# Rows of ones made pair by pair, batch 1 prepared from step 0 on, and the last experts' first weights loaded inside attention

## The reference

```
x = x + 0.5 * ffn(layernorm(x))     # first expert phase
x = x + attn(layernorm(x))
x = x + 0.5 * ffn(layernorm(x))     # second expert phase, same weights
```

## Time and profile before

| | us |
|---|---|
| median of 3 runs | 2451.97 |
| runs | 2429.93 to 2452.05 |
| profiled execution | 2452.92 |
| its span, first to last instruction | 2451.1 |
| TensorE busy | 2177.5 (89%) |
| VectorE, ScalarE, GpSimd busy | 1740.6, 1730.3, 976.2 |
| mean granted TensorE clock | 0.91 |

### The profile page before, as it was taken

One profiled execution on the slowest core, in us unless ns is written; L12 is line 12 of the kernel. 1 busy time (PEld: TensorE's weight loads), 2 busy tenths in 40 slices (PEclk: granted clock), 3 DMA queues, 4 the chain that ended last, 5 costly groups with the idle time before them and its releaser, 6 DMA issues.

```text
span 2451.1 us, 36414 instructions
## 1 busy us (share of the span) xinstructions
PE 2177.5 (89%) x12974; PEld 1153.8 (47%) x12974; DVE 1740.6 (71%) x2555; ACT 1730.3 (71%) x3390; POOL 976.2 (40%) x1157
## 2 busy tenths in 40 slices
PE   5749964579999999999999999999999999964997
PEld 5748853344344434434443443444444334224896
DVE  5636754368888888798888778878888988203774
ACT  5846654128888788788878878877887877634663
POOL 3754512271264256239227514832741111112442
PEclk8569986569999999999999999999999999666998
DMA  5725420514235334344333444432362340103431
GB/s 201 264 88 181 152 73 35 103 35 96 54 64 120 58 76 105 71 58 105 97 57 85 101 76 73 90 94 37 84 122 41 78 62 16 51 9 130 139 121 61
DMA packets 144901, 218.29 MB, mean 89 GB/s; under 512 B 32224, under 2 KB 100954, under 8 KB 144464
## 3 DMA queue, kind: packets, MB, share of 16 engines
q1 hardware_dynamic: 135504, 199.01, 34.6%
q0 software_dynamic: 9216, 16.95, 2.0%
HBM read 129.59 MB, written 84.80 MB: 87 GB/s over the span
## 4 chain that ended last, share of the span: by engine, by line
PE 73%; DVE 10%; POOL 5%; ACT 5%; issue 4%; DMA 2%; SPq 0%; POOLq 0%; DVEq 0%; ACTq 0%
PE PS L780 18%; PE PS L764 17%; PE PS L747 11%; PE PS L692 6%; DVE NMX L1302 5%; PE PS L568 4%; PE PS L724 3%; POOL buf L1425 2%; PE PS L661 2%; PE PS L662 2%; PE PS L663 2%; PE PS L645 2%; PE PS L647 2%; PE PS L600 2%; PE PS L646 2%
## 5 line engine op out<-in xcount | busy, mean ns | idle before, releaser
L1302 DVE TENSOR_REDUCE NMX<-PS 128x1 f32<-128x1024 f32 x1024 | 1224.5, 1219 | 300.7 <-PE PS L747 294.9
L998 ACT ACTIVATE PB<-PS 128x512 f32<-128x512 f32 x2048 | 1103.4, 605 | 250.9 <-PE PS L764 243.4
L764 PE MATMUL PS<-QF,KF 51*128 51x512 f32 x2048 | 814.6, 473 | 12.1 <-ACT PB L998 7.4
L747 PE MATMUL PS<-KF,QF 49*128 49x512 f32 x2048 | 725.1, 451 | 47.8 <-DVE NMX L1302 35.6
L764 PEld LDWEIGHTS PS<-QF,KF 51*128 51x128 f32 x2048 | 334.8, 189 | 573.6 <-ACT PB L998 292.8
L780 PE MATMUL PS<-PB,V 128*17 128x512 f32 x4096 | 559.4, 619 | 0.2
L747 PEld LDWEIGHTS PS<-KF,QF 49*128 49x128 f32 x2048 | 315.7, 190 | 181.9 <-DVE NMX L1302 116.1
L1406 POOL TENSOR_TENSOR RS<-VE,NEGH 128x8 f32<-128x8 f32 x24 | 40.2, 1676 | 404.8 <-DVE VE L1096 404.8
L1229 DVE TENSOR_TENSOR HLR<-HL,HHR 128x512 fp32r<-128x512 f32 x128 | 88.7, 693 | 91.8 <-ACT HHR L928 91.8
L661 PE MATMUL PS<-W2H,HLR 128*128 128x256 f32 x512 | 142.8, 279 | 0.0
L663 PE MATMUL PS<-W2H,HHR 128*128 128x256 f32 x512 | 141.5, 276 | 0.0
(11 more groups left out here) (171 smaller groups left out, 3303.5 us busy)
## 6 DMA issues: line engine op xcount, KB each, us to landing
W<-in_w SPq DMA_DIRECT2D x32, 1024.0 KB, 8.1
QF<-qs SPq DMA_DIRECT2D x192, 128.0 KB, 4.7
KF<-qs SPq DMA_DIRECT2D x192, 128.0 KB, 7.5
qs<-HI SPq DMA_DIRECT2D x64, 256.0 KB, 2.1
qs<-R1R SPq DMA_DIRECT2D x64, 256.0 KB, 2.4
buf<-ZT SPq DMA_DIRECT2D x16, 520.0 KB, 9.9
BUF<-buf SPq DMA_DIRECT2D x16, 520.0 KB, 8.4
PX<-x2d SPq DMA_DIRECT2D x8, 1024.0 KB, 5.5
```

Source lines behind the costliest of these rows:

```text
L747: m = e.matmul(PS[:, 2 * i + half, :], QF[k][at:at + ROWS_S, p * SEQ + ti * 128:p * SEQ + ti * 128 + 128], KF[k][at:at + ROWS_S, p * SEQ + ...
L764: e.matmul(PS[:, bank, :], KF[k][at:at + ROWS_ST, p * SEQ + sbk * 128:p * SEQ + sbk * 128 + 128], QF[k][at:at + ROWS_ST, p * SEQ + th * 51 ...
L998: e.activation(PB[j % 3][:, h * 512:(h + 1) * 512], PS[:, place["e", tile], :], ACT.Exp).then_inc(e_out, 1)
L1302: e.tensor_reduce(NMX[:, u % 2, at:at + 1], PS[:, 2 * i:2 * i + 2, :], AX.XY, ALU.max, negate=True).then_inc(s_max, 1)
```

## The change

1. Ones. The three pairs get their rows from a generator `ones()`: pair 0 at once, pairs 1 and 2 in step 60 of batch 0's preparation. `load_unit(u)` waits for the ones of its own pair instead of `load_unit(0)` for all. The memsets of V17 write the 17th column only.
2. Batch 1. All engines begin its preparation with base 0 instead of -12. Its `load_unit(4)` comes in step 53 instead of 52.
3. Weights. SP issues `load_w(8)` and `load_w(9)` in step 492, after waits for all users of the scratch under them. ScalarE and VectorE convert W1 and W2 of expert 8 in step 534 (ScalarE behind a wait for the last `weigh`) instead of after the loop and at the head of `experts(1)`.

The diff, cut to its core (the line for batch 1 stands the same way in TensorE's, ScalarE's, VectorE's and GpSimd's programs):

```diff
                 if u >= 3:
                     e.wait_ge(e_full, 64 * (u - 2))
+                else:
+                    e.wait_ge(set_act, 2 * u + 2)
...
                 if b:
-                    yield EARLY + 52
+                    yield EARLY + 52 if b > 1 else 53
                     load_unit(4 * b)
...
-            e.wait_ge(set_act, 6)
             load_unit(0)
             for n in range(NS + LAST + 1):
                 b, r = divmod(n, BATCH)
                 if n == 0:
-                    side.begin(-EARLY, before(1))
+                    side.begin(0, before(1))
...
                 side.run(n)
-
-            e.wait_ge(e_out, 64 * NU)
-            e.wait_ge(pv_full, 16 * NU)
-            e.wait_ge(rope_out, 8 * NB)
-            load_w(NE)
-            load_w(NE + 1)
+                if n == NS - 20:
+
+                    e.wait_ge(sq_sum, 8 * NB)
+                    e.wait_ge(rope_out, 8 * NB)
+                    e.wait_ge(sp_full, 8 * NB)
+                    for i in range(2):
+                        e.wait_ge(st_q[i], 128 * NB)
+                    load_w(NE)
+                    load_w(NE + 1)
             experts(1)
...
                 if n == 0:
-                    prepare(side, -EARLY, 1, pre_x, values, split)
+                    prepare(side, 0, 1, pre_x, values, split)
...
-                if ph:
-                    split_w2(NE)
                 gathered(NE * ph)
...
-            for k in range(3):
-                for t in (QF[k], KF[k]):
-                    e.copy(t[32:64, :], ONES[32:64, 0:1].to_broadcast([32, 2048]))
-                    e.copy(t[96:128, :], ONES[96:128, 0:1].to_broadcast([32, 2048])).then_inc(set_act, 1)
+            def ones():
+                for k in range(3):
+                    for t in (QF[k], KF[k]):
+                        e.copy(t[32:64, :], ONES[32:64, 0:1].to_broadcast([32, 2048]))
+                        e.copy(t[96:128, :], ONES[96:128, 0:1].to_broadcast([32, 2048])).then_inc(set_act, 1)
+                    yield VALUES_AT[3] + 1
+
+            side.begin(0, ones())
             prepare(side, 0, 0, pre_x, values, split)
...
                 side.run(n)
-
-            e.wait_ge(pv_full, 16 * NU)
-            split_w1(NE)
+                if n == NS + LAG + LATE:
+
+                    e.wait_ge(pv_full, 16 * NU)
+                    split_w1(NE)
+                    split_w2(NE)
+
...
-            own.out(e.memset(V17[0][:, :, :, :], 1.0))
-            own.out(e.memset(V17[1][:, :, :, :], 1.0))
+            own.out(e.memset(V17[0][:, :, :, 16:17], 1.0))
+            own.out(e.memset(V17[1][:, :, :, 16:17], 1.0))
...
-            split_w1(NE)
+                if n == NS + LAG + LATE:
+                    split_w1(NE)
+                    split_w2(NE)
+
```

More of the change, by code:

```diff
@@ L1347, in vector_program @@
                 if n == 0:
-                    prepare(side, -EARLY, 1, pre_x, split)
+                    prepare(side, 0, 1, pre_x, split)
                 if r == BATCH - EARLY and b + 2 < NB:
```

## The result

| | before | after |
|---|---|---|
| median of 20 runs, us | 2449.5 | 2423.1 |
| runs, us | 2429.9 to 2452.4 | 2404.9 to 2433.1 |
| ratio after / before, 95% interval | | 0.9887 (0.9865 to 0.9909) |
| profiled execution, us (span) | 2452.9 (2451.1) | 2421.0 (2419.2) |

The median falls by 26 us. The runs of a kernel fall into two groups some 20 us apart, and this must be seen first, since it is where about half of the gap comes from. Before: 19 runs at 2446.7 to 2452.4 (mean 2449.7) and one at 2429.9. After: 11 runs at 2421.0 to 2433.1 (mean 2428.0) and 9 at 2404.9 to 2409.7 (mean 2408.0). Upper against upper and lower against lower, the kernels differ by about 22 us.

The account below looks back on a forecast made before the run. TensorE was taken as 73% of the chain of waits, so gains come only where it stands still. Terms -11.3 - 22.0 + 10.3 + 9 + 2.5 - 3.0 - 1.3 + 1.0 = -14.8, from 2452.9 to 2438 us; range 2421 to 2449.

Parts of the forecast that it names:

- rival (a): Step 36: GpSimd finishes the split before SP needs it, so no new wait for MT; 2426.6 us, chance 0.12.
- the 1% that was called likeliest: Whole kernel: a change within about 1% (24.5 us, line at 2427.5) counts as the same; chance 0.73.
- Ones: Start of batch 0's preparation: eight of twelve copies leave ScalarE's queue head, which then waits for GpSimd; gain 11.3 us.
- Fill: Steps 0 to 19 of attention: 65.1 us instead of 87.05 with batch 1 prepared later, -22.0.
- the 20 x 2.53: Steps 0 to 19: twenty undisturbed steps of 2.53 us each, paced by two 1.2 us maxima on VectorE.
- Moved work, stop and clock: Behind the fill: six projections and two splits +10.3, SP's queue stopping TensorE in step 36 +9, low clock +2.5.
- (c): After the stop in step 36 the clock does not come back; slower, 2483 us, chance 0.05.
- Weights and passage: Passage into the second expert phase, weights loaded in step 492: scatter -3.0, BUF -1.3, reciprocal's store +1.0.
- Scatter: Passage: the last scatter, no longer beside the weight loads, lands in 2.8 us instead of 5.85; -3.0.
- BUF: Passage: the BUF load took 5.32 us; between 0 and half of it gained, taken as -1.3.
- RC's store: Step 534: conversion ahead of unit 31's reciprocal delays its store from 2180.84 to 2181.9; +1.0.
- If the changed kernel's median falls there: Rival: whole at another level, likeliest place the last 20 steps at low clock; 2416 us, chance 0.10.

Follow-up runs that it names:

- experiment 5: Ones alone, and batch 1's preparation from step 0 alone, each on the kernel before with idle score matmuls (chip B): 2436.7 and 2437.9 us.
- experiment 3: Changed kernel with one store of batch 1's preparation (split half 0, j = 1) due one step later, chip A: 2426.15 us.
- experiment 4: Changed kernel with idle matmuls, batch 1 at base 4: 2416.4 us (chip B); with batch 2's x2 load also three steps later, no stop: 2388.85 us (chip C).
- Experiment 1: Four idle matmuls per step, steps 513 to 531, added to before and changed kernels: 2427.5 and 2406.5 us (chip A), 2426.2 and 2406.9 (chip C).

## Why the prediction was right or wrong

The size was wrong: 14 us below the median of before were forecast, 26 measured. The median lies in the range, but by luck: the range reached down that far for rival (a), no wait for MT, and the wait came. The measured ratio of 0.9887 lies past the 1% that was called likeliest, though the interval (up to 0.9909) does not exclude it.

**Ones**, forecast -11.3: -11.0 (100.2 to 89.2). ScalarE waits for GpSimd as said, and the moved copies cost nothing (experiment 5: steps 0 to 63 unchanged).

**Fill**, forecast -22.0: -25.0. Mis-sized were the terms around the 20 x 2.53. The load and statistics lengthened steps 0 to 4 by 3.2 us, not 4.4. The transposes lengthened steps 9 to 12 by 1.9, not 4.35, because VectorE's maxima pace these steps and TensorE has room beside them: I charged TensorE's time in a stretch that I had myself called paced by VectorE. The projections took 6.5, not 5.7.

**Moved work, stop and clock**, forecast 10.3 + 9 + 2.5 = 21.8: steps 20 to 63 are 21.8 longer. The stop is 8.45, the low clock behind it 3.2 (steps 36 to 39, 14.6 against 11.4 in experiment 3), which leaves 10.1 for the moved work. The kernel of experiment 4 without a stop supports it: 12.0 for eight projections and two splits, where these terms give 11.2. The Trainium skill ("TensorE: Matmul & The Clock Gate", Terms) puts the penalty of a low clock at the throttled time times the share of clock lost. A mean of 0.66 over 12.00 us puts 8.2 us at the low level, so by that rule the penalty is an estimated 4.1. The trace gives less (3.2); what makes up the difference no run shows. Rivals (a), no wait, and (c), the clock that stays low, are out: it was back at 576.8, 9 us after the stop had ended. Nor is their sum what the removal of the wait brings: without it (experiment 3) another took its place, and 3.8 of these 11.7 us were won.

**Weights and passage**, forecast -3.3: -4.9 in the profiled pair, -3.9 with the level held, -3.5 alone. Scatter -3.75 for -3.0, BUF -1.5 for -1.3, RC's store +0.7 for +1.0.

These make -18 to -19.5 for -14.8. **The step that failed** is the other one: "If the changed kernel's median falls there ... Nothing in the change argues for it. Chance 0.10." The forecast took the low clock of the earlier trace rows as a fixed property of both kernels and set its sum against 2452. The runs showed that it changes from execution to execution of the same kernel. One of the three runs shown lay 22 us lower, the prediction even named the place and priced it (25 us; 24.4 between the profiled before and the held clock), and then gave the whole of it, all or nothing, one chance in ten. A third of the runs in another group means that a median can land anywhere between the groups. With the mix open, the forecast would have run from 2438 down to 2416 around 2427. Experiment 1 shows the clock to be the cause of the groups; that the change itself moves the mix is neither shown nor excluded (lower group in 9 of 20 runs against 1 of 20 in the first table, but on chip A in 4 of 12 with its loads against 16 of 29 without).

## What to carry to other kernels

Where the runs shown have two groups, forecast each group and the mix, and compare changes with whatever makes the groups held still: here four idle matmuls per step turned a comparison of medians that mixed 19 to 22 us of change with 4 to 7 of the mix into one that is good to a few us, on two of the three chips. And where periodic work is moved in an in-order queue, keep its place within the period: base 0 for base -12 met the queue's other periodic items, load_max(1), then load_unit(3) and gather(0); base 4, the same place modulo 16, met only one at the seam to the next batch.

## What the runs showed of the hardware

TensorE's clock fell once within the last 20 steps, where scores and maxima have ended and weights, exp and values go on, at 11, 30, 40 and 53 us behind the start of step 511 in four traces (before, loads alone, after, experiment 3), and did not come back before the loop's end. From step 511 to the last YU copy these took 82.2, 73.2, 67.3 and 60.2 us, against 57.8 with the clock held: what a fall costs depends on how early it comes, so the upper group is a spread and not one level, and the last of the four belongs to a run of the lower group. At the low clock the step took 4.04 instead of 2.59 us, a factor of 1.56 and not of two: in the profiled after TensorE is busy 82% of 2104.0 to 2119.5, at the high level, and 95% of 2120 to 2146, at the low one.

On chip B every profile shows a slower stretch in steps 451 to 455, and every one a pause of ScalarE of 2.3 us, ended 15 us behind the start of step 511 with no releaser in this core, with a clock that fell 1 to 2 us later and stayed low for 7 to 38 us although the idle matmuls ran. From the timeline of ACT with the ones alone:

```profile
2104.13 1.08 ACT L1005 ACTIVATE PB<-PS 128x512 f32<-128x512 f32 x2 [2.33 <-remote]
```

Step 511 to the last YU copy took 62.7 us there with the ones alone and 76.5 in the changed kernel, against 57.8 on chips A and C. So idle matmuls hold the clock against the lack of work, not against such a pause. What pauses the engine is open, and so is whether the pause or something behind it makes the clock fall.
